# A gated linear recurrence: the outputs' sums inside half a chunk moved to TensorE, the sums across halves made block-diagonal, and one chain of sums per step

## The reference, cut to what matters

```python
def step(St, inp):
    kt, qt, vt, at, bt = inp
    Sk = jnp.einsum('bhij,bhj->bhi', St, kt)
    err = Sk - vt
    Sn = at[..., None] * St - (bt[..., None] * err)[..., None] * kt[:, :, None, :]
    ot = jnp.einsum('bhij,bhj->bhi', Sn, qt)
    return (Sn, ot)
```

## Time and profile before

| what | us |
|---|---|
| median of 3 runs | 3094.34 |
| profiled execution, its own time | 3091.77 |
| its span, first to last instruction | 3090.1 |
| VectorE busy | 2235.5 |
| TensorE busy | 2079.5 |
| ScalarE busy | 1170.6 |

### The profile page before, as it was taken

The page is one execution under the profiler, slowest core; times in us unless marked ns, Lnnn a source line. Parts: engine busy times, 40 slices in busy tenths (PEclk is TensorE's granted clock), DMA queues, the critical chain, the costliest instruction groups (busy, mean ns, idle before and its releaser), DMA issues. The chain is left out here.

```text
span 3090.1 us, 43379 instructions
## 1 busy us (share of the span) xinstructions
PE 2079.5 (67%) x12498; PEld 1439.8 (47%) x12498; DVE 2235.5 (72%) x5902; ACT 1170.6 (38%) x2868; POOL 826.9 (27%) x804
## 2 busy tenths in 40 slices
PE   8999999954666666666654545599968462389800
PEld 4555555524554545454443434478843341157600
DVE  5878777769999999999999988655628483023334
ACT  2555555534555555555443435333300110122200
POOL 1444444440111011100011110044435117411175
PEclk8999999977777777777776667799989565679955
DMA  3666666552566677788999991323220602048732
GB/s 93 121 121 119 120 121 121 119 138 57 142 163 162 177 187 202 207 224 236 256 262 256 269 291 46 129 81 94 75 80 22 223 7 80 2 129 260 227 101 85
DMA packets 660490, 448.38 MB, mean 145 GB/s; under 512 B 291344, under 2 KB 607551, under 8 KB 654025
## 3 DMA queue, kind: packets, MB, share of 16 engines
q1 hardware_dynamic: 551083, 314.96, 39.9%
q0 software_dynamic: 29600, 87.09, 9.3%
q10 hardware_dynamic: 79616, 44.06, 4.9%
HBM read 244.49 MB, written 207.77 MB: 146 GB/s over the span
## 5 line engine op out<-in xcount | busy, mean ns | idle before, releaser
L561 DVE SCALAR_TENSOR_TENSOR p_zo<-p_w,p_gd,p_zo 128x128 f32<-128x128 f32 x2304 | 649.5, 347 | 11.3
L384 DVE SCALAR_TENSOR_TENSOR p_y<-p_ps_proj,p_w,p_y 128x508 f32<-128x508 f32 (+2 forms) x576 | 416.0, 741 | 115.0 <-ACT p_y L298 101.5
L864 PE MATMUL p_ps_z<-p_turned,p_gcol 112*32 112x128 f32 x3584 | 229.2, 417 | 384.3 <-DMA p_turned<-history 381.3
L864 PEld LDWEIGHTS p_ps_z<-p_turned,p_gcol 112*32 112x32 f32 x3584 | 139.5, 159 | 470.3 <-issue 300.9
L847 PE MATMUL p_ps_x<-p_w,p_diag_o 128*128 128x128 f32 x2048 | 302.8, 296 | 67.6 <-ACT p_diag_o L885 26.1
L234 PE MATMUL p_ps_proj<-p_x,p_w 128*128 128x512 f32 x768 | 343.0, 596 | 2.7 <-ACT p_beta_t L289 2.7
L885 ACT ACTIVATE p_diag_o<-p_ident,p_gd 128x128 f32<-128x128 f32 x1024 | 314.0, 388 | 60.6 <-PE p_ps_x L847 53.9
L847 PEld LDWEIGHTS p_ps_x<-p_w,p_diag_o 128*128 128x128 f32 x2048 | 259.6, 200 | 110.8 <-ACT p_diag_o L885 67.4
L829 PE MATMUL p_ps_x<-p_w,p_diag_z 128*128 128x128 f32 x1536 | 214.9, 300 | 94.8 <-DVEq L581 44.2
L706 POOL DMA_DIRECT2D p_dec<-decays x32 | 17.6, 550 | 975.0 <-DVEq L665 761.7
L898 ACT ACTIVATE p_diag_z<-p_ident,p_gd 128x128 f32<-128x128 f32 x768 | 232.8, 388 | 95.4 <-PE p_ps_x L829 69.5
(11 more groups left out here) (213 smaller groups left out, 3375.2 us busy)
## 6 DMA issues: line engine op xcount, KB each, us to landing
history<-p_hist SPq DMA_DIRECT2D x18, 2048.0 KB, 14.3
gram<-p_gram SPq DMA_DIRECT2D x64, 512.0 KB, 5.4
history_sums<-p_sums ACTq DMA_DIRECT2D x112, 256.0 KB, 5.8
p_zo<-history_sums SPq DMA_DIRECT2D x28, 1024.0 KB, 7.9
p_wgu<-in_wguT SPq DMA_DIRECT2D x64, 352.0 KB
decays<-p_dec SPq DMA_DIRECT2D x64, 256.0 KB, 2.3
beta_v<-p_bv SPq DMA_DIRECT2D x64, 256.0 KB, 2.5
p_dec<-decays POOLq DMA_DIRECT2D x32, 512.0 KB, 6.1
```

The lines of the kernel that those rows point to most:

```text
L384: nc.vector.scalar_tensor_tensor(out=yv[:, :, s:], in0=pv[:, :, 0:T - s], scalar=par[j % 2][:, kind, TAPS - 1 - s:TAPS - s], in1=yv[:, :, ...
L561: return done(nc.vector.scalar_tensor_tensor(out=acc, in0=row, scalar=scalar, in1=acc, op0=ALU.mult, op1=ALU.add))
L864: last = nc.tensor.matmul(ps_z[k % NZ][h * 2 * C:(h + 1) * 2 * C, u % UB * QUADS + q, :], gcol[u % NTURN][:, q * 4 + h, :], turned[u % NTU ...
```

## The change

Only the recurrence is rewritten, in these parts:

- z stays on VectorE: in each step one chain of sums over the half's earlier rows (the constant `CHAINS = HALF` leaves a second, side chain unused). The rows of a step go into one of two new tiles (`ws`), not back in place, so that TensorE can still read the old ones.
- o inside a half goes to TensorE: for each step s, `own_rows` multiplies k+1 rows by k+1 diagonals from ScalarE (two buffers of four) and adds them up in PSUM, and after four steps adds the scaled earlier part by one matmul with the identity. ScalarE copies the result back (`finished`).
- z and o across the halves: GpSimd's queue moves the first half's rows into `near_w` with (head, step) in the partitions (8 DMAs, `send_rows`) and the gram numbers into a block-diagonal matrix `near_g` (32 DMAs, `load_near`); TensorE multiplies, one matmul a sequence and kind (`near_product`), ScalarE copies, TensorE turns the result back by 8 transposes (`near_turn`), and VectorE adds it.
- the 16 units of the history of a leaf stand between the steps of the next leaf in TensorE's order: 0, 0, 1, 2, 2, 2, 3, 3 of them behind the steps of the first half, the last three behind the near products. The buffers `sums` and `ps_z` are two each instead of four.

```diff
-    NZ = 4
+    NZ = 2
+    NS = 2
...
+    DO = 4
+    NDO = 2
+    NW = 2
...
+    CHAINS = HALF
+    UNITS_AFTER = (0, 0, 1, 2, 2, 2, 3, 3)
...
-                            if r < 0:
-                                o_at = mul(zo[g][:, 1, s - 1, :], zo[g][:, 1, s - 1, :], w[g][:, 0, :])
-                            else:
-                                o_at = add_scaled(zo[g][:, 1, s - 1, :], w[g][:, 1 + r, :], gd[g][:, r, C + s - 1:C + s])
...
+                    if k == 0 and at + half:
+                        dve.wait_ge(pair_mm, pairs_at(at, s) - HALF)
+                    elif 2 <= k < HALF - 1:
+                        dve.wait_ge(pair_mm, pairs_at(at, s - 1))
+                    if k:
+                        after(max(w_at, u_at))
+                        w_at = mul(new[:, 0:k, :], old[:, 0:k, :], dec[half][:, k:k + 1, :].broadcast_to([P, k, DH]))
...
+                    for r in range(k):
+                        if k >= CHAINS and r % 2:
...
+                        else:
+                            after(z_at)
+                            z_at = add_scaled(z, old[:, r, :], gram(half, r, s))
...
+                for q in range(2):
+                    dve.wait_ge(x_done, at * BANKS + q + 1)
+                    rows = slice(HALF + q * 4, HALF + q * 4 + 4)
+                    z_at = add(zo[g][:, 0, rows, :], zo[g][:, 0, rows, :], ps_x[:, q])
...
+            def send_rows(at):
...
+                pool.wait_ge(half_done, at + 1)
...
+                for b in range(BG):
+                    pool.dma_start(near_w[:, b, :], w[g][b * H:(b + 1) * H, 1:1 + HALF, :]).then_inc(near_in[b // ZB], DMA)
...
+            def own_rows(at, s):
...
+                pe.wait_ge(step_done, rows_at(at, s))
...
+                for r in range(k + 1):
...
+                    pe.wait_ge(diag_o_made, p // DO + 1)
+                    nc.tensor.matmul(ps_o[s // 4 % 2][:, s % 4, :], diag_o[p // DO % NDO][:, p % DO, :], rows[:, r, :],
+                                     start=(s % 4 == 0 and r == 0), stop=False).then_inc(pair_mm, 1)
...
+            for at in range(LEAVES):
...
+                for s in range(HALF):
+                    own_rows(at, s)
+                    while u < min(units, sum(UNITS_AFTER[:s + 1])):
+                        history(at - 1, u)
+                        u += 1
+                pe.wait_ge(near_g_in, (at + 1) * 2 * H * DMA)
+                near_product(at, 0)
+                near_turn(at, 0)
+                near_product(at, 1)
+                while u < units:
+                    history(at - 1, u)
+                    u += 1
+                near_turn(at, 1)
+                for s in range(HALF, C):
+                    own_rows(at, s)
...
+                act.wait_ge(mm_done, (k + 1) * UB)
+                if k >= NS:
+                    act.wait_ge(z_out[k % NS], k // NS * DMA)
+                nc.scalar.copy(sums[k % NS][:], ps_z[k % NZ][:]).then_inc(z_cp, 1)
```

More of the change, by code:

```diff
@@ L458, in recurrence @@
         w = [m.sb(f"p2_w{g}", [P, C + 1, DH]) for g in range(GR)]
+        ws = [m.sb(f"p2_ws{i}", [P, HALF - 1, DH]) for i in range(NW)]
         pp = m.sb("p2_pp", [P, HALF, DH])
@@ new lines, in leaf @@
+                p_at = w_at = u_at = o_at = 0
+                for k in range(HALF):
+                    p_at, w_at, u_at = step(0, k, p_at, w_at, u_at)
+                    if k % 4 == 3:
+                        after(p_at)
+                        if k == HALF - 1:
+                            after(u_at)
+                            dve.sem_inc(half_done, 1)
+                        rows = slice(k - 3, k + 1)
+                        o_at = mul(zo[g][:, 1, rows, :], zo[g][:, 1, rows, :], pp[:, rows, :])
+                        assert base + o_at == scaled_at(at, k // 4)
@@ new lines, in leaf @@
+                after(z_at)
+                dve.sem_inc(x_read, 1)
+                w_at = u_at = 0
+                p_at = z_at
+                for k in range(HALF):
+                    p_at, w_at, u_at = step(1, k, p_at, w_at, u_at)
+                    if k == 3:
+                        dve.wait_ge(x_done, at * BANKS + BANKS)
+                        for q in range(2):
+                            rows = slice(HALF + q * 4, HALF + q * 4 + 4)
+                            o_at = add(zo[g][:, 1, rows, :], zo[g][:, 1, rows, :], ps_x[:, q])
+                        after(o_at)
+                        dve.sem_inc(x_read, 1)
+                        o_at = mul(zo[g][:, 1, HALF:, :], zo[g][:, 1, HALF:, :], pp[:])
+                        assert base + o_at == scaled_at(at, 2)
@@ new lines, in _ @@
+                sp.dma_start(by_seq(g, c * C + HALF, HALF), w[g][:, 1 + HALF:, :]).then_inc(u_saved[g], DMA)
+                sp.wait_ge(u_saved[g], (c + 1) * 2 * DMA)
+                for u in range(NTURN):
+                    if not c:
+                        load_rows(u, 0, known)
+                    load_rows(u, known, rows)
+                for u in range(NTURN, UNITS):
+                    load_columns(u)
+                    load_rows(u, 0, rows)
+                sp.wait_ge(o_out[g], (c + 1) * DMA)
@@ L869, in _, with history @@
-            cross_o(NCHUNK - 1, 0)
-            cross_z(NCHUNK - 1, 1)
-            cross_o(NCHUNK - 1, 1)
+            pe.wait_ge(cleared, 2 * NTURN + 3)
+            def history(at, u):
+                n = at * UNITS + u
+                k = n // UB
+                pe.wait_ge(turned_in[n % NTURN], loads(n) * DMA)
+                if k >= NZ:
+                    pe.wait_ge(z_cp, k - NZ + 1)
+                for q in range(QUADS):
+                    for h in range(4):
+                        last = nc.tensor.matmul(ps_z[k % NZ][h * 2 * C:(h + 1) * 2 * C, u % UB * QUADS + q, :],
+                                                gcol[n % NTURN][:, q * 4 + h, :], turned[n % NTURN][:, q * 4 + h, :],
+                                                start=True, stop=True)
+                last.then_inc(mm_done, 1)
@@ L935, in _, with past @@
-            for u in range(DUNITS):
-                diagonal_z(NCHUNK - 1, 1, u)
-            diagonals_o(NCHUNK - 1, 1)
+            made = 0
+            for at in range(LEAVES):
+                units = UNITS if 0 < at <= ROUNDS * GR else 0
+                b = 0
+                def past(s, made):
+                    half, k = divmod(s, HALF)
+                    until = min((at * 2 + half) * (PAIRS // DO) + (k + 1) * (k + 2) // 2 // DO + NDO, LEAVES * 2 * PAIRS // DO)
+                    for n in range(made, until):
+                        diagonals(n)
+                    if s % 4 == 3:
+                        finished(at, s // 4)
+                    return max(made, until)
+                if 0 < at <= (ROUNDS - 1) * GR:
+                    keep(at - 1)
+                for s in range(HALF):
+                    made = past(s, made)
+                    while (b + 1) * UB <= min(units, sum(UNITS_AFTER[:s + 1])):
+                        batch_row(at - 1, b)
+                        b += 1
+                near_rows(at, 0)
+                near_rows(at, 1)
+                while b * UB < units:
+                    batch_row(at - 1, b)
+                    b += 1
+                for s in range(HALF, C):
+                    made = past(s, made)
```

537 lines of the change are left out of this document (234 added, 303 removed).

## The result

The changed kernel takes 3058.12 us (median of five runs, 3047.3 to 3070.8) beside 3089.1 us for the kernel before on the same chip (3087.59 to 3095.97). The ratio is 0.9894, with an interval of 0.9857 to 0.993: faster by 1.1%. The forecast was 2977 us, a ratio of 0.962. So some 31 us came where 117 were expected. The profiled execution was the fastest of the five. It has a span of 3045.6 us against 3090.1 before; a last store at 1923.87 against 1969.10 says that its recurrence is 45 us shorter.

A forecast was written before the change was run, and what follows sets the result against it. VectorE's instruction list was taken to set 15 of 16 leaves, with DMA engines and SyncE's queue close behind. Leaf terms summed to 1168 us against 1285, a gain of 117: 2977 us, range 2905 to 3055.

The forecast's parts named there:

- VectorE's list: VectorE's own instructions in a leaf: 51.7 us against 70.0 in leaf 0, with chained sums at 0.388 us each.
- The first half: VectorE's first half of a leaf waits at step 6 for pairs behind history units, ending at 25.2 instead of 21.8 us.
- The path of the near rows: Between the halves, GpSimd's DMAs, landing, matmuls, copy and transposes: 11.8 us together, 3.3 of it after the landing.
- The failed step: In SyncE's cycle, last units wait for near sums, there at +37 early; last copy at +43 to +49, rounds 2 to 6.
- Waits inside a half: VectorE waiting for TensorE's order: +3.4 us in the first half and +3.8 in the second.
- The price of a pair: On TensorE, eight pairs cost 2.4 us, from matmuls at 0.296; a history unit costs 1.02 us.
- The lockstep rival: ScalarE and TensorE don't overlap on diagonals: a pair costs 0.7 us, a leaf 80, about 3180 us; chance 0.14.
- SyncE's cycle: SyncE's queue goes through a leaf's history in order: cycles of 64, 71, 76.5, 84 and 90 us in rounds 2 to 6.
- The rival in which SyncE's cycle is stretched whole: Second load of sums comes 9 to 13 us later every round, nothing behind it shrinks: 3035 us; chance 0.2.
- The DMA term: The new DMAs add about 3 us a leaf to the DMA engines, busy for 83 of 87 us in leaf 13.
- The ends: First and last leaves: leaf 0 ends at 752, as now; leaf 14 takes 65 us, leaf 15 59 and 6 more.
- The signs the prediction named: Wrong if VectorE waits for pairs in most steps, rounds 1 and 2 leave 60 to 72 us, or DMA share falls below 0.85.

The follow-up runs named there:

- diag2x4: The changed kernel with four diagonal buffers of two instead of two of four (same memory): 2994.21 us, ratio 0.987.
- before_t3: The kernel before with three load buffers for the history's units instead of four: 3061.62 us beside 3029.06, ratio 1.0104.

## Why the direction was right and the size wrong

- **VectorE's list: right.** Seven chained sums take 2.67 us, (2.67 - 0.35)/6 = 0.387 each (0.388 forecast from the earlier trace rows). VectorE is busy for 50.65 us in leaf 3, in round 1; the forecast was 51.7 with 2 us of waits in it, and 2.2 of history. Leaf 0 ends at 745.6, 6 us before the forecast 752; its first half is done at 711.05, forecast 715, since its wait for the identity is 9.2 us and not 11.5. The price of a chained sum stands as the prediction had it. Its sentences on the rule of the Trainium skill ("VectorE: DVE Perf Modes", The DRAIN you can't avoid) leave out what the same section adds, that a next operation which isn't held starts earlier. With that, 0.262 us for two chains in turn is no disagreement.
- **The first half: the number right, the place of the wait wrong.** +25.7 in leaf 3, forecast +25.2. But the wait in it stands at step 5 and not at step 6, so it is in part luck that the two agree to 0.5 us: it is 4.58 us for the pairs of step 3, which stand behind unit 0, and that waits 6.58 us for its load.
- **The path of the near rows: right while it runs.** GpSimd is released 0.35 us behind the half, its 8 DMAs take 4.20 us, and from the first near product to VectorE's addition it is 3.55 (925.50 to 929.05), forecast 3.3.
- **The failed step: "the last three units wait for the near sums, which are there at +37 in early rounds … the last copy is at +43, +44, +45, +47, +49".** In leaf 3 the near sums came at +44.8 and the last copy at +48.7 from the start of the leaf (932.9), and the last copies are at +46.9 in leaf 1 and +59 in leaves 13 and 14. For the near sums it put only the row loads and hand-overs behind the first half, so that TensorE's units 7 to 12 had to be done by then. That took the times at which units arrive from the trace of before, where four buffers load ahead. The changed kernel has three, and holds them longer, because pairs stand between the units. It is shown from both sides: the buffer cut alone makes the kernel before 1.0% slower, and given back it brings the changed kernel from 0.9894 to 0.9672 (with smaller groups of diagonals, whose 0.0024 is inside the noise, and a later load of the gates, whose share is not known), its last copies to +41.5…+44 in leaves 1 to 6 and its cycles to a sum of 979 us, where the forecast's own terms say 968. Between forecast and result lie 0.027; this step is 0.022 of it by that pair, and the store of the next point 0.009 to 0.012. They are more than the gap together, so other terms were too long: with both mended and two chains the thirteen cycles sum to 955 us, 13 under the forecast. That four buffers alone come within 11 us of it is in part luck.
- **What was left out beside it: the store of the outputs.** The prediction counted the new DMAs and moved none of the old ones. The store of 1 MB goes out at +15 instead of +29. Moving it back brings 0.0116 with three buffers and 0.0088 with four. It collides with the unit loads: TensorE's wait for them falls from 295.5 to 250.4 us, and unit 4 of leaf 3 is there 2.9 us behind its issue instead of 5.9. Whether the store's bytes or its number of pieces does it is open; a store of fewer bytes was not run.
- **Waits inside a half: right in early leaves.** The forecast had 3.4 + 3.8 us a leaf for pairs; measured are 5.7 to 8.2 in leaves 1 to 6, though in other places. Of the 192.5 us in all, 10 are leaf 0's, and 89 are the wait at step 5 in leaves 7 to 14, behind unit 0: it grows from 5.4 to 17.6 us as the queue falls behind VectorE (16.59 in leaf 13). That is the queue's cycle seen from VectorE, not the price of pairs.
- **The price of a pair: too low, and of a unit too high.** A pair takes 0.394 us and not 0.296, a unit 0.71 and not 1.02. Both are the clock and not a hand-over: pairs took 0.396 us with the smaller groups of `diag2x4` as well, and TensorE waited for ScalarE's diagonals three times, 28.2 of 29.3 us in one place. The cross sums before stood in a row, at a granted clock of 0.92 in leaf 4 (1032.5 to 1054), and the units behind waits for loads, at 0.57 (987 to 1011); now they stand among each other. The lockstep rival, in which ScalarE holds TensorE, is ruled out by the same rows.
- **SyncE's cycle: right as a mechanism.** From round 3 on the queue no longer waits for the leaf's end, and in leaf 13 it is 14.6 us behind VectorE (1684.56 against 1670.0). Its length was off by the same late copy: the save of the decayed history is at +66 in leaf 13, forecast about +58. The rival in which SyncE's cycle is stretched whole (3035, chance 0.2) came closest to the time, and to the cycles of rounds 3 to 6: it had 78, 84, 89, 94, measured are 78.1, 82.0, 89.3, 93.1 in the mean of each pair. It names the same queue; its cause, a late second load of sums, follows at least in part from the buffers and the store. The 1.5 and 2 us that the prediction added for ScalarE's two buffers were nothing: of 110.5 us before ScalarE's copies 109.9 are waits for TensorE, and TensorE's 295.6 before the units are all but 0.1 waits for loads.
- **The DMA term: near.** 3 us a leaf were taken. DMA engines were busy for 949 us in leaves 1 to 14 together, before for 881: 4.9 a leaf.
- **The ends.** Leaf 14 lasts to 1864.0, 82.6 us after the last save instead of 65, since the queue enters it late; leaf 15 takes 57.5. Cycles +68, leaf 14 +17.6, leaf 0 and leaf 15 -14: together 72 us, which is what the profiled execution has over the forecast.
- **The signs the prediction named.** It said it would be wrong if VectorE waited for pairs in most steps, if leaves of rounds 1 and 2 left 60 to 72 us, or if the DMA share fell below 0.85 in round 6. There are 49 waits for pairs in 16 leaves, three a leaf of 16 steps, and the DMA share of leaf 13 is 0.94. But of the leaves of rounds 1 and 2 three are near the upper edge (69.6, 70.9, 69.0) and leaf 5 is over it (72.5): this sign did show. The near-sum wait, forecast none from round 3 on, is there in every leaf.

With four buffers the wait for pairs is still 200 us, and for the same reason: 6.1 to 7.9 us in leaves 1 to 6, and 115 us at step 5 in leaves 7 to 14, where SyncE's queue is behind. What stays open: how much of the fourth buffer's gain is the later load of the gates, how much of two chains' gain is the clock, and, since the changed kernel was not run on the chips of the experiments, the third digit of every difference against 0.9894.

## What to carry to other kernels

Where transfers are paced by buffers, the time at which the n-th one arrives belongs to the number of buffers, to what holds them and to what else is under way, and not to the transfer alone. A trace of before gives those times only for its own ring: read every constant of the diff that sizes a ring before taking an arrival time from it, and when consumers of the ring are interleaved with other waits, count one full round trip for every ring's length of units (here an estimate of 7 us beside the store, 5.9 from the issue to the multiplication and 1.1 of matmuls, and 4 us without it). A large store that moves by 15 us is part of the change, even if none of its lines are touched.

## What the runs showed of the hardware

- A unit of the history, two DMAs, took 5.9 us (leaf 3) and 7.1 us (leaf 4) from its first issue to its multiplication with a store of 1 MB under way, and 2.9 us in leaf 3 with that store moved. Cutting its rows from 32 to 16 took 1.0 and 1.9 us from the cycles of leaves 3 and 4 (69.9 and 67.1 against 70.9 and 69.0), moving the store 5.2 and 1.4 (65.7 and 67.6). Over these two leaves, moving the store was worth more than halving the rows of the loads (6.6 against 2.9 us).
- Pairs of the same shape took 0.27 us each at a granted TensorE clock of 1.00 and 0.49 at 0.50, the clock's two levels (2.4 and 1.2 GHz).
- GpSimd takes as long to issue a DMA of 64 pieces of 32 bytes as one of 128 pieces of 512 bytes: 284.2 us over 512 is 0.555 each for the gram numbers, 67.1 over 128 is 0.524 for the near rows (4.20 us for the eight of leaf 3).
- The kernel before took 3089 to 3092 us in two of the comparisons and 3029 to 3033 in the three others, 2% apart, as much as most of the effects here. The difference lies behind the recurrence: from the last store of its outputs to the end it is 1119 to 1122 us in the three profiles of the slower chips and 1058 to 1072 in the eleven others. In the recurrence no such difference is seen, by an estimate: the kernel before takes 3029.1 us on the chip of `before_t3`, and that run takes 1737.4 outside its recurrence, which leaves 1292 for the recurrence, beside 1291 on a slower chip. Whole times from different chips can't be compared; ratios can, and so can the recurrence by itself.
